# Last stage of a graph network kernel: x3 is added on TensorE, statistics and new rows read PSUM, and ScalarE and VectorE work in another order

## What is computed

```python
def _gat_forward(x, edge_index, qw, kw, ln_gamma, ln_beta, out_w, out_b):
    row, col = (edge_index[0], edge_index[1])
    Q = jnp.einsum('nf,hfd->hnd', x, qw)
    K = jnp.einsum('nf,hfd->hnd', x, kw)
    Qr = Q[:, row]
    alpha = jnp.einsum('hed,hed->he', Qr, K[:, col]) / scale
    ...
    a = a / denom[:, col]
    msg = Qr * a[..., None]
    agg = jax.vmap(lambda m: jax.ops.segment_sum(m, col, num_segments=n))(msg)
    h = jnp.transpose(agg, (1, 0, 2)).reshape(n, HEADS * HID)
    mu = jnp.mean(h, axis=-1, keepdims=True)
    var = jnp.mean((h - mu) ** 2, axis=-1, keepdims=True)
    h = (h - mu) / jnp.sqrt(var + EPS) * ln_gamma + ln_beta
    h = h * jax.nn.sigmoid(h)
    return h @ out_w + out_b
...
x = _layernorm(x + _L3_gnn_ref(x, edge_index, ...), axis=-1)
```

## Time and profile before

| | us |
|---|---|
| median of 3 runs | 2939.72 (2933.82 to 2942.26) |
| the profiled execution | 2922.87 |
| its span, first to last instruction | 2921.2 |
| last stage, from its first product with alpha | 2540.5 to the end, 380.7 |
| engines busy in the span | PE 61%, DVE 80%, ACT 60%, POOL 58% |
| mean granted TensorE clock | 0.793 of full speed |

### The profile page before, as it was taken

How to read it: one execution, slowest core, us unless ns; L and a number is a source line. 1 busy time by engine, 2 the same in 40 slices (tenths; PEclk the granted TensorE clock), 3 DMA queues, 4 the chain that set the end, 5 groups by cost and what they waited for, 6 DMA issues and landing times.

```text
span 2921.2 us, 51701 instructions
## 1 busy us (share of the span) xinstructions
PE 1794.2 (61%) x9573; PEld 1388.7 (48%) x9573; DVE 2325.5 (80%) x9167; ACT 1748.5 (60%) x4457; POOL 1696.6 (58%) x1605
## 2 busy tenths in 40 slices
PE   5666666466666644777777666657775666455552
PEld 4555555355555532554455333335654555343331
DVE  7878777898898856878887788858886999887773
ACT  3545544322322225888887688855556888588874
POOL 7777777346666664333332666647766766156664
PEclk8777777688888877989998899979997888655555
DMA  6777777434444436999998798958886888544441
GB/s 183 233 234 233 239 236 223 159 77 78 78 80 78 81 35 230 356 331 343 353 348 309 256 304 300 304 191 263 260 262 222 295 294 293 176 148 141 141 140 50
DMA packets 280171, 625.34 MB, mean 214 GB/s; under 512 B 51230, under 2 KB 84649, under 8 KB 280055
## 3 DMA queue, kind: packets, MB, share of 16 engines
q1 hardware_dynamic: 207543, 523.73, 52.5%
q0 software_dynamic: 72512, 100.52, 15.5%
HBM read 342.76 MB, written 285.23 MB: 215 GB/s over the span
## 4 chain that ended last, share of the span: by engine, by line
DVE 18%; ACT 13%; issue 12%; PE 7%; DMA 7%; DVEq 2%; POOL 1%; SPq 1%; ACTq 0%; POOLq 0%
ACT node_out L1244 7%; DVE n_stats L1537 4%; DMA acc_dump<-acc 3%; DMA node_in<-in_x_dram 3%; PE ps L1077 2%; DVE acc L1590 2%; ACT node_x2t L1244 2%; PE ps L1197 2%; DVE fix_acc L2058 1%; DVE node_in L1970 1%; DMA node_in<-y_nodes 1%; PE ps L1088 1%; DVE node_in L2120 1%; DVE pre L2078 1%; ACT node_x2t L1337 1%
## 5 line engine op out<-in xcount | busy, mean ns | idle before, releaser
L1244 ACT ACTIVATE node_out<-node_in,n_shift,n_root 128x128 f32<-128x128 f32 (+1 forms) x1176 | 468.1, 482 | 81.3 <-DVE n_shift L1554 81.3
L786 POOL DMA_INDIRECT sums<-gat_sums,dst_safe_i x196 | 185.9, 948 | 290.9 <-DVE pre L1970 235.9
L903 POOL DMA_INDIRECT out_dram<-node_x2t,out_index x196 | 210.6, 1074 | 192.7 <-ACT node_x2t L1244 126.1
L794 POOL DMA_INDIRECT src_rows<-x_table,row_i x200 | 199.8, 999 | 127.2 <-issue 54.2
L794 POOL DMA_INDIRECT sums<-x_table,row_i x192 | 194.8, 1015 | 87.8 <-issue 49.7
L786 POOL DMA_INDIRECT src_rows<-in_x_dram,src_i x196 | 195.6, 998 | 84.8 <-issue 82.7
L849 POOL DMA_INDIRECT gat_sums<-src_rows,add_idx x100 | 160.1, 1601 | 141.0 <-ACT src_rows L1316 45.6
L1537 DVE BATCH_NORM_STATS2 n_stats<-node_in 128x6 f32<-128x256 f32 (+1 forms) x588 | 209.3, 419 | 20.3 <-DMA node_in<-y_nodes 9.3
L794 POOL DMA_INDIRECT own_rows<-in_x_dram,dst_safe_i x196 | 190.7, 973 | 59.8 <-issue 56.4
L1026 PE MATMUL ps<-alpha,node_in 128*128 128x196 f32 x392 | 118.0, 467 | 171.0 <-DVE junk L1860 167.8
L1253 ACT ACTIVATE t_a<-ps 128x512 f32<-128x512 f32 (+1 forms) x198 | 115.8, 585 | 162.4 <-PE ps L948 162.1
(11 more groups left out here) (413 smaller groups left out, 6579.9 us busy)
## 6 DMA issues: line engine op xcount, KB each, us to landing
own_rows<-x_table SPq DMA_DIRECT2D x245, 256.0 KB, 3.0
node_in<-in_x_dram SPq DMA_DIRECT2D x96, 512.0 KB
x_table<-node_out SPq DMA_DIRECT2D x96, 512.0 KB
x_table<-new_rows SPq DMA_DIRECT2D x147, 256.0 KB
gat_sums<-node_x2t SPq DMA_DIRECT2D x49, 528.0 KB, 4.3
acc_dump<-acc SPq DMA_DIRECT2D x98, 264.0 KB
node_sums<-gat_sums SPq DMA_DIRECT2D x48, 528.0 KB
h_table<-node_h SPq DMA_DIRECT2D x48, 512.0 KB
```

The costliest lines, as they stand in the source:

```text
L786: g_.indirect_dma_start(out=to[:, g.b, j, 0:width], out_offset=None, in_=tab, in_offset=bass.IndirectOffsetOnAxis(ap=indices(j), axis=0)). ...
L794: g_.indirect_dma_start(out=to4[g.q][:, j, 0:F], out_offset=None, in_=tab, in_offset=bass.IndirectOffsetOnAxis(ap=indices(j), axis=0)).the ...
L903: g_.indirect_dma_start(out=out[:, :], out_offset=bass.IndirectOffsetOnAxis(ap=out_index[:, t:t + 1], axis=0), in_=wide_new[:, g.b, j, :], ...
L1244: last = sc.activation(to[0:pn, g.b, j, :], rows[0:pn, g.b, j, 0:F], ACT.Identity, bias=NORM[k][2][0:pn, g.b, j:j + 1], scale=root[0:pn, j ...
```

## The change

x3 is no longer added on VectorE: TensorE adds it in PSUM as a product with the identity matrix, between bias and product, and bias and x3 of the first bank stand ahead of the wait for silu. The statistics of x4 and the new rows read PSUM, and node_y is not used. PSUM is free again when the new rows are done. The x3 rows' buffer is free when the product is done. ScalarE's order becomes roots, silu of the step two behind, new rows, normalised rows; VectorE's becomes product with alpha, inverses and shifts, seven sums in a row, attended rows, statistics of x4.

```diff
--- before.py
+++ after.py
@@ -472,7 +472,7 @@
                          rings=dict(own=1, stored=1), quads=dict(quad=J)),
             "nodes4": dict(front=norm("n") + ["n_pre", "n_row"], rings=dict(n_in=1, n_out=1), steps=DENSE_STEPS),
             "att2": dict(front=["msgd"],
-                         back=["accd", "rcp", "rcp2", "pre", "msg0", "tr_a", "cp_a", "mm", "pre2", "newd"]
+                         back=["accd", "rcp", "rcp2", "pre", "msg0", "tr_a", "cp_a", "mm", "newd"]
                          + norm("n") + norm("a"),
                          rings=dict(qin=1, own=1, dumped=1, scattered=WJ), steps=WIDE_STEPS, per=dict(accd=WJ)),
         }
@@ -735,7 +735,7 @@
                 sp.dma_start(wide_rows(acc_dump, ACC_W, g), wide_acc[g.b][:, 0:WJ, :]).then_inc(L["dumped"].sems[g.b], 16)
 
             def load_x3(g):
-                wait_free(sp, L["pre2"], g)
+                wait_free(sp, L["mm"], g)
                 sp.dma_start(wide_own[g.b][:, 0:WJ, :], wide_rows(x3_table, F, g)).then_inc(L["own"].sems[g.b], 16)
 
             pipeline(sp, WIDE_STEPS, wide_edges((0, load_q), (1, dump_wide), (1, load_x3)))
@@ -1198,13 +1198,18 @@
                 last.then_inc(L["tr_a"].sem, 1)
 
             def att_project(g, jn=WJ):
-                wait_done(pe, L["cp_a"], g)
-                wait_free(pe, L["pre2"], g)
+                wait_free(pe, L["newd"], g)
+                if g is not WIDE_FIX:
+                    wait_landed(pe, L["own"], g)
                 for lo in range(0, jn, J):
                     n = min(J, jn - lo)
                     bank = ps[2 + g.b][lo // J]
+                    own = fix_own[:, 0, :] if g is WIDE_FIX else wide_own[g.b][:, lo:lo + n, :].rearrange("p j f -> p (j f)")
                     te.matmul(bank[:, 0:n * F], ones_bf[:, :], outb_parts[:, 0:n, :].rearrange("p j f -> p (j f)"),
                               start=True, stop=False)
+                    te.matmul(bank[:, 0:n * F], ident[:, :], own, start=False, stop=False)
+                    if lo == 0:
+                        wait_done(pe, L["cp_a"], g)
                     for j in range(n):
                         last = te.matmul(bank[:, j * F:(j + 1) * F], wide_t[g.b][:, (lo + j) * F:(lo + j + 1) * F], outw_sb[:, :],
                                          start=False, stop=j == n - 1)
@@ -1434,16 +1439,20 @@
                 last.then_inc(L["cp_a"].sem, 1)
 
             normed_tiles = normed_rows(L, "n", node_h1, node_out, "msg0", None, ("tr_a",))
-            new_x4_tiles = normed_rows(L, "a", node_y, wide_new, "newd", "scattered")
 
             def normed(g, jn=WJ):
                 normed_tiles(g, jn)
 
             def new_x4(g, jn=WJ):
-                new_x4_tiles(g, jn)
+                wait_drained(act, L["scattered"], g)
+                wait_done(act, L["a_nm"], g)
+                for j in range(jn):
+                    last = sc.activation(wide_new[:, g.b, j, :], ps[2 + g.b][j // J][:, j % J * F:(j % J + 1) * F], ACT.Identity,
+                                         bias=NORM["a"][2][:, g.b, j:j + 1], scale=NORM["a"][1][:, g.b, j:j + 1])
+                last.then_inc(L["newd"].sem, 1)
 
             att_root, x4_root = roots(L, "n"), roots(L, "a")
-            pipeline(act, WIDE_STEPS, wide_edges((3, x4_root), (1, att_root), (3, new_x4), (1, normed), (1, silu)))
+            pipeline(act, WIDE_STEPS, wide_edges((3, x4_root), (1, att_root), (2, silu), (3, new_x4), (1, normed)))
             att_root(WIDE_FIX, 1)
             normed(WIDE_FIX, 1)
             silu(WIDE_FIX, 1)
@@ -2207,47 +2216,15 @@
                 wait_done(dve, L["pre"], g)
                 moments((L, "n", g, node_h1, P, DJ if jn == WJ else jn))
 
-            def x4_sums(g, jn=WJ):
+            def x4_pairs(g, jn=WJ):
+
+
                 wait_done(dve, L["mm"], g)
-                wait_free(dve, L["newd"], g)
-                if g is not WIDE_FIX:
-                    wait_landed(dve, L["own"], g)
-                for lo in range(0, jn, J):
-                    n = min(J, jn - lo)
-                    own = fix_own[:, 0, :] if g is WIDE_FIX else wide_own[g.b][:, lo:lo + n, :].rearrange("p j f -> p (j f)")
-                    last = v.tensor_tensor(node_y[:, g.b, lo:lo + n, :].rearrange("p j f -> p (j f)"), ps[2 + g.b][lo // J][:, 0:n * F],
-                                           own, ALU.add)
-                last.then_inc(L["pre2"].sem, 1)
-
-            def x4_half(lo):
-
-                def add(g):
-                    if lo == 0:
-                        wait_done(dve, L["mm"], g)
-                        wait_free(dve, L["newd"], g)
-                        wait_landed(dve, L["own"], g)
-                    n = min(J, WJ - lo)
-                    made = v.tensor_tensor(node_y[:, g.b, lo:lo + n, :].rearrange("p j f -> p (j f)"), ps[2 + g.b][lo // J][:, 0:n * F],
-                                           wide_own[g.b][:, lo:lo + n, :].rearrange("p j f -> p (j f)"), ALU.add)
-                    if lo:
-                        made.then_inc(L["pre2"].sem, 1)
-                return add
-
-            def x4_pair(j):
-
-
-                def make(g):
-                    if j == 0:
-                        wait_done(dve, L["pre2"], g)
-                        wait_free(dve, L["a_nm"], g)
-                    made = v.bn_stats(NORM["a"][0][:, g.b, j:j + 2, :].rearrange("p j c -> p (j c)"),
-                                      node_y[:, g.b, j:j + 2, :].rearrange("p j f -> p f j"))
-                    if j == DJ - 2:
-                        made.then_inc(L["a_bn"].sem, 1)
-                return make
-
-            def x4_variances(g):
-                variances(L, "a", g, P, DJ, NORM["a"][1][:, g.b, :])
+                wait_free(dve, L["a_nm"], g)
+                for j in range(0, DJ if jn == WJ else jn, 2):
+                    last = v.bn_stats(NORM["a"][0][:, g.b, j:j + 2, :].rearrange("p j c -> p (j c)"),
+                                      ps[2 + g.b][j // J][:, j % J * F:(j % J + 2) * F].rearrange("p (j f) -> p f j", f=F))
+                last.then_inc(L["a_bn"].sem, 1)
 
             def inverses(k):
 
@@ -2265,19 +2242,17 @@
                 return make
 
             def x4_moments(g, jn=WJ):
-                wait_done(dve, L["pre2"], g)
-                moments((L, "a", g, node_y, P, DJ if jn == WJ else jn))
+                x4_pairs(g, jn)
+                variances(L, "a", g, P, DJ if jn == WJ else jn, NORM["a"][1][:, g.b, :])
 
             att_shifts, x4_shifts = shifts(L, "n"), shifts(L, "a")
             sums_of = [(0, wide_sum(j)) for j in range(WJ)]
             pipeline(dve, WIDE_STEPS, wide_edges(
-                (3, inverses("a")), (1, inverses("n")), (3, shift_only("a")), (1, shift_only("n")),
-                (0, attended_rows), sums_of[0], sums_of[1], (2, x4_half(0)), sums_of[2], (2, x4_half(J)), sums_of[3], (2, x4_pair(0)),
-                sums_of[4], (2, x4_pair(2)), sums_of[5], (2, x4_pair(4)), sums_of[6], (2, x4_pair(6)), (2, x4_variances), (0, attended)))
+                (0, attended_rows), (3, inverses("a")), (1, inverses("n")), (3, shift_only("a")), (1, shift_only("n")),
+                *sums_of, (0, attended), (2, x4_moments)))
             fix_sums(L, ACC_W, 4, wide_acc[WIDE_FIX.b][:, 0, :], WJ)
             attended(WIDE_FIX, 1)
             att_shifts(WIDE_FIX, 1)
-            x4_sums(WIDE_FIX, 1)
             x4_moments(WIDE_FIX, 1)
             x4_shifts(WIDE_FIX, 1)
```

## The result

Both kernels in turn on one chip, four runs each: before 2936.77 us (2933.79 to 2942.26), after **2895.84** (2884.33 to 2899.34), ratio 0.9852, 95% interval 0.9818 to 0.9885: faster by 41 us. On a later chip, with six runs of after: 2937.55 and 2903.68, ratio 0.9873 (0.9843 to 0.9902), 34 us. I had said 2916, and 2905 to 2932.

The account below looks back on a forecast made before the run. No engine was full; an order of waits, ScalarE's 12.06 us step, set the pace. 22 looped steps falling to 11.15 us gave 20.0, unrolled steps 4: 24 us off the 2939.7 median, 2916, range 2905 to 2932.

Parts of the forecast that it names:

- The step that failed: Last stage: the root's table load, 1.28 us, follows x4's variance, so the root ends 1.6 us after it.
- the chain of 11.5: Looped step at 1.2 GHz: root's table and roots 1.7, silu's table 1.3, silu 1.36, TensorE 5.45, statistics 1.63, hand-overs 0.1.
- VectorE's sum: Looped step: shifts done at 2.15 us, sums at 5.8, attended block at 9.3, x4's statistics and variance at 11.0.
- The mean of the two levels: Looped step: TensorE's clock levels taken in turn, 11.5 us at 1.2 GHz and 11.0 at 2.4, put at 11.15.
- The wait of 1.98: ScalarE in before's loop: idle until TensorE's transposes finish; some 0.3 of the 1.98 us was to stay.
- Rivals C: x4 statistics on VectorE: each pays a part more for reading PSUM, 0.35 us a step; 2923 us, chance 0.08.
- E: x4 statistics: strided PSUM read at half rate, TensorE warm, VectorE's loop 12.4 us; 2943, no change, chance 0.11.
- rival B: Last stage: TensorE stays at 1.2 GHz, 11.5 us a step; 2924 us, chance 0.20.
- the new loop of waits: Last stage: silu, product, statistics and root follow one another, 11.5 us a step at 1.2 GHz.
- the rest of the stage: Unrolled steps, three ahead of the loop and one behind: 1 us gained each, 4 together.
- Rival D: VectorE's sums run 0.39 us apart, not 0.51; 10.5 us a step with late products, 2902 us, chance 0.06.
- Rival F: New loop of waits decides if TensorE's part plus statistics exceed 7.1 by 0.5 us; slower, 2956 us, chance 0.06.

Follow-up runs that it names:

- e3b: After, with a second wait for x4's variance ahead of its root, so the root's table load stands behind it; profiled again: 2918.79 us, single run.
- e12: Before, with silu's two waits exchanged, the one for the transposes last: 2925.08 us, ratio 0.9935.
- e13: After with ScalarE's old order (roots, new rows, normalised rows, silu of the step one behind) and silu's two waits exchanged: 2910.99 us, ratio 0.9892.
- e10: After itself, unchanged, run again in five rounds on one chip: 2903.68 us, ratio 0.9873 to before.
- e5: After, with VectorE's steps written out instead of looped, the other engines keeping their loops: 2886.49 us, ratio 0.9815 to before.
- e1: Before, with ScalarE's new order alone, the x3 adds staying on VectorE: 3015.57 us, ratio 1.0262.

## Why the prediction was wrong

The direction was right, and so was the mechanism as far as it goes: silu's wait leaves, and VectorE's own work takes over. One step of the working was wrong, and it decides the size.

- **The step that failed:** "The root's table and the root end at 0.1 + 1.28 + 0.23 = 1.6", and with it "root's table and roots 1.7" in the chain of 11.5. The load lies ahead of the wait. Without 1.28 the chain is 10.2 at 1.2 GHz; the unrolled steps measured 10.08. In VectorE's sum the root no longer counts, for the product with alpha ends later; the sums start 1.78 us behind the variance (2745.44 to 2747.22) where I had 2.25. They took 3.39 for my 3.57, and the whole is 10.25 for my 11.0 (rounded up from 10.9). To that comes what I had not counted, the loop's turn of 0.56 in every second step: 10.53, measured 10.60. Against 11.15 that is 0.55 a step, 12 us over the loop. e3b puts the load where I had it and gets 11.24.
- **The mean of the two levels.** 11.0 and 11.5 make 11.25, not the 11.15 that I used. That is 2 us over the loop, and the slip brought the forecast nearer to the result.
- **The same oversight stood in my reading of before.** The wait of 1.98 is not the transposes' alone: with the load ahead of the wait it is 0.62, and a step 10.89 (e12). So most of what the new order gains in the loop, by taking silu off that wait, the exchange of two waits gains as well: with it the old order (e13) runs at VectorE's 10.6 too. What remains in after's favour are the unrolled steps, 9.4 to 10.1 (after, e10) against 11.1 to 11.8 (e13).
- **Right:** silu's wait gone, the wait for the variance new. Reading PSUM costs nothing: over the whole stage the 113 statistics from PSUM average 420 ns, those from SBUF 419. The Trainium skill ("VectorE: DVE Perf Modes", TRN2 errata) would have it 62 cycles dearer; the measurement disagrees and decides. Rivals C and E fall with it. TensorE's clock, forecast at 0.6 to 0.8, was 0.74, and rival B falls; even at the lower level the new loop of waits, 10.08 us, is shorter than VectorE's 10.6. TensorE's part was 5.2 to 5.4 for 5.45. SP's loads cost nothing that shows: in the loop TensorE and VectorE wait for no DMA.
- **Luck:** the rest of the stage, 4.1 for 4. I gave each unrolled step the loop's gain of 1 us, but their table load had never stood behind the transposes, and they gained 0.7 each; what follows the loop, 2.4 for 1, made it up.
- **Rival D** named nearly the right step (10.5) for the wrong reason: the sums in the loop stand 0.50 apart, not 0.39. e5 has the spacing that D described, and its loop's turn is gone too.
- **Rival F**, slower through the new loop of waits, needed TensorE's part and the statistics half a microsecond above 7.1; they came to 6.8, and the chain had 1.3 us more room than I thought. e1 shows that such a loop is real: the same order with the adds in their old place is 2.6% slower.
- **The median.** I took the saving off the median of the runs, which was the right base: the profile of before was 14 us under it, and its stages ahead of the change ended 10 us or more earlier than in every other profile used here.

What stays open: why the stages ahead end up to 25 us apart from one profile to another with the same code (2545.1 to 2570.0), and why the sums stand further apart in a hardware loop.

## What to carry to other kernels

Before pricing a wait ahead of an activation that changes the table, see in the compiled order on which side of it the table load stands; with silu's two waits, the one written first stood ahead of the load in the loops, and behind it in the unrolled steps, in before and in e12 alike. Where the same step runs at two paces in looped and unrolled code, ask why first: here exchanging two waits alone gave 1.17 of the change's 1.46 us a looped step. And compare the stage that a change touches between two profiles, not their spans.

## What the hardware showed that I had not expected

- A table load behind a wait adds its 1.28 us to the path, one ahead of the wait runs while ScalarE waits anyway: 11.24 against 10.60 us a step (e3b, after), 12.06 against 10.89 (before, e12).
- More matmuls made TensorE faster: 0.75 of full speed granted with those of x3, 0.54 without, at the same pace.
- The same dependent sums stand 0.50 us apart in a hardware loop and 0.40 written out, and a turn of the loop costs VectorE 0.56.
- Seven activations of 128 x 128 take 2.56 us from PSUM and 2.80 from SBUF.
